# Four GNN layers on one core: the edge sort's unpacking on GpSimd, its tile comparison in bf16 pairs, a class table of its own, two hot rows on VectorE, and another order on TensorE

## The reference

```python
edge_index = jnp.stack([src, dst])
x = x + L0(relu(ln(x)), edge_index, edge_attr_32, edge_type_2, edge_weight)   # attention
x = x + L1(relu(ln(x)), src, dst)                                             # softmax-weighted sum
x = x + L2(relu(ln(x)), edge_index, edge_attr_2)                              # two-layer MLP, batch norm
x = x + L3(relu(ln(x)), edge_index, edge_type_16)                             # message and update
# L2: h = concat([x[row], x[col], edge_attr]) @ W1 + b1, segment_sum over row
# L3: m = relu(concat([x[src], emb[edge_type]]) @ W.T + b), segment_sum over dst
```

## Time and profile before

| | |
|---|---|
| median of 3 runs | 4499.23 us (4487.35 to 4502.24) |
| span of the profiled execution | 4484.2 us |
| the sort's loop in it, first L2859 to the flag | 1888 to 2386 us |
| of these 498 us: PE / DVE / ACT / POOL busy | 311.0 / 461.5 / 384.8 / 0 us |
| granted TensorE clock there, share of 2.4 GHz | 0.77 |

### The profile page before, as it was taken

One profiled execution on the slowest core, in us unless ns is written; L12 is line 12 of the kernel. 1 busy time (PEld: TensorE's weight loads), 2 busy tenths in 40 slices (PEclk: granted clock), 3 DMA queues, 4 the chain that ended last, 5 costly groups with the idle time before them and its releaser, 6 DMA issues.

```text
span 4484.2 us, 86419 instructions
## 1 busy us (share of the span) xinstructions
PE 3388.1 (76%) x31445; PEld 2760.2 (62%) x31445; DVE 3298.9 (74%) x6627; ACT 2085.6 (47%) x6042; POOL 1894.4 (42%) x2179
## 2 busy tenths in 40 slices
PE   1388888778989863266663778868699999869996
PEld 1155555545555542166663678855599999859995
DVE  5477776657777754599995887776766666779997
ACT  2355555545666532288883557660222222234443
POOL 0366677757777751000000210000255555548884
PEclk6688898889999976677876889989899999989998
DMA  4666676667777740100001220114244443223332
GB/s 96 210 189 182 189 201 188 188 165 203 223 210 215 211 119 14 39 9 12 12 10 32 90 68 38 46 46 158 82 126 126 125 127 125 88 68 128 129 128 67
DMA packets 382872, 524.57 MB, mean 117 GB/s; under 512 B 78756, under 2 KB 309862, under 8 KB 382304
## 3 DMA queue, kind: packets, MB, share of 16 engines
q1 hardware_dynamic: 328287, 354.60, 26.1%
q0 software_dynamic: 54144, 164.25, 12.9%
HBM read 407.61 MB, written 111.07 MB: 116 GB/s over the span
## 4 chain that ended last, share of the span: by engine, by line
PE 35%; DVE 28%; POOL 14%; issue 9%; ACT 7%; DMA 3%; another core or an unknown queue 2%; SPq 2%; DVEq 0%; POOLq 0%; ACTq 0%
POOL arena_a L1191 11%; PE psum L3700 5%; PE psum L3716 4%; PE psum L3651 4%; PE psum L3649 4%; PE psum L3003 3%; POOL arena_c L1229 2%; ACT arena_c L2966 2%; PE psum L3616 2%; PE psum L3675 2%; PE psum L3288 2%; PE psum L3698 2%; DVE arena_a L3196 2%; PE psum L3647 2%
## 5 line engine op out<-in xcount | busy, mean ns | idle before, releaser
L1191 POOL DMA_INDIRECT arena_a<-src_table,src_tix x808 | 820.4, 1015 | 459.8 <-issue 380.6
L3420 POOL TENSOR_SCALAR node_hot<-arena_c 128x128 fp32r<-128x128 f32 x575 | 369.4, 653 | 900.7 <-DVE arena_c L3308 568.0
L3438 DVE SCALAR_TENSOR_TENSOR msg_parts<-psum,msg_parts 128x512 fp32r<-128x512 f32 (+2 forms) x644 | 425.2, 660 | 260.5 <-ACT msg_parts L3587 228.3
L3138 POOL TENSOR_SCALAR node_hot_dst<-arena_c 128x128 fp32r<-128x128 f32 x587 | 383.9, 671 | 122.1 <-DVE arena_c L3542 67.6
L3587 ACT ACTIVATE msg_parts<-psum 128x512 fp32r<-128x512 f32 (+2 forms) x325 | 186.4, 574 | 520.6 <-PE psum L3651 520.6
L3003 PE MATMUL psum<-arena_a,arena_c 128*128 128x150 f32 x1800 | 288.7, 330 | 173.7 <-ACT arena_c L2969 173.7
L3649 PE MATMUL psum<-arena_c,arena_a 128*128 128x128 bf16 x3675 | 406.4, 220 | 0.0
L3651 PE MATMUL psum<-arena_c,arena_a 128*128 128x128 bf16 x3675 | 406.4, 220 | 0.0
L3003 PEld LDWEIGHTS psum<-arena_a,arena_c 128*128 128x128 f32 x1800 | 283.1, 224 | 176.8 <-ACT arena_c L2969 176.8
L3128 POOL TENSOR_SCALAR arena_a<-arena_a,arena_c 128x2500 bf16<-128x2500 bf16 x8 | 60.0, 7500 | 709.0 <-DMA arena_a<-bucket_lists 709.0
L1371 ACT ACTIVATE arena_c<-psum 128x272 f32<-128x272 f32 x404 | 151.4, 393 | 432.2 <-remote 233.8
(11 more groups left out here) (594 smaller groups left out, 10190.3 us busy)
## 6 DMA issues: line engine op xcount, KB each, us to landing
y_rows<-arena_c SPq DMA_DIRECT2D x101, 576.0 KB
arena_a<-bucket_rows SPq DMA_DIRECT2D x150, 384.0 KB
arena_b<-near_keys SPq DMA_DIRECT2D x101, 252.0 KB
arena_a<-bucket_rows SPq DMA_DIRECT2D x50, 448.0 KB
arena_a<-bucket_lists SPq DMA_DIRECT2D x25, 896.0 KB
pair_counts<-arena_c SPq DMA_DIRECT2D x25, 800.0 KB
arena_a<-bucket_lists SPq DMA_DIRECT2D x25, 704.0 KB
arena_a<-src_table,src_tix POOLq DMA_INDIRECT x808
```

What stands on the lines that cost most here:

```text
L1191: e.indirect_dma_start(out_, None, table, bass.IndirectOffsetOnAxis(ap=idx, axis=0)).then_inc(sem, 16)
L3138: return e.tensor_scalar(node_hot3[at % RING_H][:, i, :], iota_row, dst_lo[:, b, t:t + 1], None, ALU.is_equal)
L3420: return e.tensor_scalar(node_hot[at % RING_M][:, i, :], iota_row, src_lo[:, b, 2 * k + j:2 * k + j + 1], None, ALU.is_equal)
L3438: e.scalar_tensor_tensor(out=to[:, 1, 0:nt, :], in0=bank[at % 4][:, 0:nt * P].rearrange("p (t f) -> p t f", f=P), scalar=0.0, in1=to[:, 0, ...
```

## The change

Five edits go together.

- `edge_table` has three words an edge (key and two attributes); the class goes to `class_table`. SP writes both, and loads both for each bucket, into `class_in` (dense) and `edge_in`. The comparison with the classes now reads `class_in`.
- The key packs its fields by 512 instead of 256. The comparison that gives `in_tile` takes bf16 inputs and output, in pairs of columns: a new small copy writes each tile number twice (`tile_pair`), and `tile_pairs` holds 1 to 50 in bf16.
- Rows 34 and 35 of `hot_pos` are written by VectorE (an equality, 128x256); ScalarE makes 34 rows and a Relu of 4352 words.
- The unpacking leaves VectorE. ScalarE copies the 150 packed words from PSUM to `packed_sb`, and GpSimd unpacks them (15 operations, division by 512 through rounding in fp32). `turned_pe` is waited for only ahead of GpSimd's last three copies.
- TensorE transposes bucket n-3 after the small products of n and ahead of the 36 products of n-1; before, it transposed n-2 behind the 36 products of n-1. The 36 products wait for `copied`, not `fields`, to reuse their bank.

```diff
-            own.step(e.tensor_tensor(member[s][:, :, 1:], bc(edge_in[b % RING_E][:, :, 0], 1, NB), bc(class_rows[:, b, :], 2, EPP), ALU.is_equal))
+            own.step(e.tensor_tensor(member[s][:, :, 1:], bc(class_in[b % RING_E], 1, NB), bc(class_rows[:, b, :], 2, EPP), ALU.is_equal))
...
-            own.step(e.tensor_tensor(in_tile, bc(tile_i, 2, KT), bc(tile_row, 1, EPP), ALU.is_equal))
+            own.mark(e.tensor_copy(tile_pair, bc(tile_i, 2, 2)))
+            e.tensor_tensor(hot_pos[s][:, ACT_HOT:, :], bc(pos_i[:, ACT_HOT:], 2, P), bc(iota_row, 1, EPP - ACT_HOT), ALU.is_equal)
+            own.settle()
+            own.step(e.tensor_tensor(in_tile.rearrange("p j (k c) -> p j k c", c=2), bc(tile_pair, 2, KT // 2), bc(tile_pairs, 1, EPP), ALU.is_equal))
...
+        def pool_unpack(e, own, b):
+            s = b % 2
+            key, attrs = packed_sb[s][:, 0:KT], packed_sb[s][:, KT:3 * KT].rearrange("p (a k) -> p a k", a=2)
+            rest = attr_rest.rearrange("p (a k) -> p a k", a=2)
+            f, kept = field[s], attr_keep[b]
+            e.wait_ge(sig.copied, b + 1)
+            own.mark(e.tensor_scalar(shifted, key, 1.0 / 512, 8388608.0, ALU.mult, ALU.add))
+            own.step(e.tensor_copy(kept[:, 0:2, :], attrs))
+            own.mark(e.tensor_scalar(above, shifted, -8388608.0, None, ALU.add))
+            own.step(e.tensor_tensor(rest, attrs, kept[:, 0:2, :], ALU.subtract))
+            own.mark(e.tensor_scalar(shifted, above, 1.0 / 512, 8388608.0, ALU.mult, ALU.add))
+            own.mark(e.tensor_scalar(end_lo, above, -512.0, -1.0, ALU.mult, ALU.add))
+            own.step(e.tensor_copy(kept[:, 2:4, :], rest))
+            own.mark(e.tensor_scalar(whole, shifted, -8388608.0, None, ALU.add))
+            own.mark(e.tensor_tensor(dst_lo[:, b, :], end_lo, key, ALU.add))
+            own.mark(e.tensor_tensor(kept[:, 4:6, :], rest, kept[:, 2:4, :], ALU.subtract))
+            own.settle()
+            own.step(e.tensor_scalar(end_hi, whole, -512.0, -1.0, ALU.mult, ALU.add))
+            own.step(e.tensor_tensor(src_lo[:, b, :], end_hi, above, ALU.add))
+            if b >= 2:
+                e.wait_ge(sig.turned_pe, b - 1)
+            e.tensor_copy(f[:, TYP, :], whole)
+            e.tensor_copy(f[:, DL, :], dst_lo[:, b, :])
+            e.tensor_copy(f[:, SL, :], src_lo[:, b, :]).then_inc(sig.fields, 1)
...
+                if 0 <= n - 2 < NB:
+                    b = n - 2
+                    s = b % 2
+                    e.wait_ge(sig.packed_pe, b + 1)
+                    if b >= 2:
+                        e.wait_ge(sig.fields, b - 1)
+                    e.activation(packed_sb[s], bank[2 + s][:, 0:3 * KT], ACT.Copy).then_inc(sig.copied, 1)
```

More of the change, by code:

```diff
@@ L677, in program @@
         restart = words(B_, 2775, [P, NB, EPP + 1])
-        in_tile = words(B_, 3700, [P, EPP, KT])
+        in_tile = words(B_, 3700, [P, EPP, KT], BF16)
+        packed_sb = [words(B_, 4600 + s * 3 * KT, [P, 3 * KT]) for s in range(2)]
+        whole, above, end_lo, end_hi, shifted = (words(B_, 4900 + i * KT, [P, KT]) for i in range(5))
+        tile_pair = words(B_, 5150, [P, EPP, 2], BF16)
+        tile_pairs = words(B_, 5190, [P, KT // 2, 2], BF16)
         RING_E = 4
-        edge_in = [words(B_, 5500 + s * 144, [P, EPP, 4]) for s in range(RING_E)]
+        class_in = [words(B_, 5500 + s * EPP, [P, EPP]) for s in range(RING_E)]
+        edge_in = [words(B_, 5644 + s * 3 * EPP, [P, EPP, 3]) for s in range(RING_E)]
+        ACT_HOT = 34
         tot = [words(B_, 6076 + s * NB, [P, NB]) for s in range(2)]
@@ L2916, in dve_sort @@
             dve_sort_lists(e, own)
-            for n in range(NB + 2):
+            for n in range(NB + 1):
                 if n < NB:
                     dve_classes(e, own, n)
-                if 0 <= n - 1 < NB:
+                if n >= 1:
                     dve_route(e, own, n - 1)
-                if n >= 2:
-                    dve_unpack(e, own, n - 2)
             e.wait_ge(sig.pre_used, NB)
@@ L2951, in pool_sort @@
             pool_gather(e, first_of, dst_keys, begin_i[0], sig.d_keys)
+            for b in range(NB):
+                pool_unpack(e, own, b)
             e.wait_ge(sig.flag, 1)
+        def pool_unpack(e, own, b):
[22 more added lines that the diff above has]
+            e.tensor_copy(f[:, SL, :], src_lo[:, b, :]).then_inc(sig.fields, 1)
         def act_sort(e):
@@ L2964, in act_sort @@
                     e.wait_ge(sig.routed, b + 1)
-                    for j in range(EPP):
+                    for j in range(ACT_HOT):
                         away = e.activation(hot_pos[s][:, j, :], iota_row, ACT.Abs, bias=minus_pos[s][:, j:j + 1])
@@ L2986, in pe_sort @@
             pause(e)
-            for n in range(NB + 2):
+            for n in range(NB + 3):
                 if n < NB:
@@ L2994, in pe_sort @@
                     e.matmul(bank[6 + s][0:1, 0:NB], ones[:, 0:1], tot[s], start=True, stop=True).then_inc(sig.pre_pe, 1)
[L2995 to L3007 removed]
+                if n >= 3:
+                    b = n - 3
                     s = b % 2
@@ L3017, in pe_sort @@
                     t_.then_inc(sig.turned_pe, 1)
+                if 0 <= n - 1 < NB:
+                    b = n - 1
+                    s = b % 2
+                    e.wait_ge(sig.spread, b + 1)
+                    e.wait_ge(sig.weighed, b + 1)
+                    if b >= 2:
+                        e.wait_ge(sig.copied, b - 1)
+                    for j in range(EPP):
+                        put = e.matmul(bank[2 + s][:, 0:3 * KT], hot_pos[s][:, j, :], routed_v[s][:, j, :, :].rearrange("p f k -> p (f k)"),
+                                       start=(j == 0), stop=(j == EPP - 1))
+                    put.then_inc(sig.packed_pe, 1)
             e.wait_ge(sig.flag, 1)
@@ L3756, in gpsimd @@
         def gpsimd(e):
-            pool_constants(e)
+            own = pool_constants(e)
             sp_wait_tables0(e)
```

77 lines of the change are left out of this document (23 added, 54 removed).

## The result

| | before | after |
|---|---|---|
| median of 4 runs | 4500.73 us (4487.35 to 4502.76) | 4426.72 us (4413.70 to 4442.63) |
| ratio after / before | | 0.9844, 95% interval 0.9809 to 0.9879 |
| span of the profiled execution | 4484.2 us | 4411.9 us |
| its part ahead of the sort | 1851.7 | 1837.1 |
| the sort, first fill of its tiles to the flag | 534.7 | 473.8 |

The change is faster, and more so than forecast: 4426.72 us is 33 us under the predicted 4460 and 7 us under the low end of the range. In the profiled execution 60.9 of the 72.3 us come from the sort. Another 14.6 come from layer 0, which the change doesn't touch; the first two experiments measure what that part does on its own.

A forecast was written before the change was run, and what follows sets the result against it. VectorE was taken to bound the sort at 18.75 us a bucket, falling to 15.5 + 1.4 = 16.9; 44.4 us gained less 5.2 lost gives 39, so 4445 for the profiled execution and 4460 for the median, range 4434 to 4492.

The forecast's parts named there:

- What bounded it before: Sort loop before the change: VectorE sets the pace at 18.75 us a bucket, with a ring close behind.
- its ring: Sort, ScalarE's rows, products, small products, VectorE over two buckets: 16.3 us a bucket before, 15.9 after without contention.
- VectorE's parts: VectorE in the sort, a bucket: 18.74 - 2.15 - 0.67 - 0.93 + 0.5 = 15.5 us if undisturbed.
- Contention: Sort, GpSimd meeting VectorE's two-input operations: nine of 15 cost VectorE 0.15 us each, 1.4 us a bucket (0.5 to 3.8).
- its rival that ended slower: Sort: each of nine meetings costs VectorE a whole GpSimd operation, 0.42 us; 19.3 us a bucket, 4517 us, chance 0.09.
- The pace: Sort after the change: VectorE is the limit at 16.9 us a bucket (16.2 to 17.6), chance 0.51.
- the first rival: Sort: no contention worth the name, the ring limits at 15.9 to 16.1 us a bucket; 60 gained, 4439 us, chance 0.18.
- ends of the loop: Sort loop's ends: unhidden unpacking of the last bucket +4.7 us, ahead of the first bucket +0.5; 5.2 us lost.
- GpSimd's operations: Unpacking on GpSimd: 11 operations at 0.39 us and 4 at 0.53, 6.4 us a bucket, 6.6 with semaphore waits.
- its upper figure of 8.8 us: GpSimd's unpacking a bucket if its five two-input operations cost twice as much.
- The sum: Whole kernel: 24 x (18.75 - 16.9) = 44.4 us gained, 5.2 lost, so 39 us gained.
- The signs named beforehand: Sort: L2871 and L2899 at 1.1 us, rows 10.04, products every 16 to 17.5, GpSimd minima near 0.39, VectorE medians 0.1 above minima.

The follow-up runs named there:

- the first two experiments: Kernel before and changed kernel, both unchanged, profiled and timed once more: 4375.73 and 4313.34 us, ratio 0.9856; sorts 534.8 and 471.8 us.
- the kernel in which GpSimd rests: Changed kernel with the same 15 unpacking operations back on VectorE, GpSimd doing nothing in the loop: 4348.92 us, ratio to before 0.9936.
- 27 no more: Changed kernel with GpSimd's 12 arithmetic operations done twice, 27 operations a bucket in place of 15: sort 513.0 us, period 17.72 us.
- one copy on ScalarE that waited for a transpose at the wrong place: Changed kernel with the transposes of bucket n-3 behind the 36 products of n-1: 4652.17 us, sort 718.8 us.

## Why the prediction was right and wrong

**What bounded it before:** right for VectorE, but a second limit was missed. The prediction gave its ring 2.4 us of slack a bucket. Another ring had hardly any: VectorE unpacked bucket b behind b's 36 products and ahead of the route of b+2. The chain of the kernel before runs through it for a while:

```profile
...
1994.18 10.64 ACT arena_c L2966 x36
2004.84 4.05 ACT arena_c L2969
2008.94 12.04 PE psum L3003 x72
2032.12 10.65 ACT arena_c L2966 x36
...
```

Between the end of the products (2021.00) and 2032.12 VectorE unpacks, compares with the classes, and routes. The 37.94 us from 1994.18 to 2032.12 are 19.0 a bucket. From 2109 to 2147 us, with shorter products, the chain is on VectorE with 18.8 us a bucket. The two limits stood side by side, and the change took the unpacking out of both.

**VectorE's parts:** right, to 0.1 us. The class comparison takes 1.09 us undisturbed (forecast 1.10), the tile comparison in bf16 1.09 (1.1), the hot rows 0.43 (0.41), L2902 5.78 (5.78). The sum of 15.5 compares with 15.47 measured, which even has the contention in it. With GpSimd at rest it is 15.14, and some 0.2 to 0.3 us of gaps between instructions come on top (17.29 of 17.56, 16.19 of 16.37 busy where VectorE is the limit).

**Contention:** wrong, and this is the step that failed. Nine meetings at 0.15 us were to cost VectorE 1.4 us a bucket; against the kernel in which GpSimd rests, 15 operations cost it 0.3 and 27 no more. From the one overlap in the earlier trace rows, where GpSimd came first with 7.09 us and VectorE lost 5.5, I took a price for each column, and charged VectorE with it in all nine. The price itself was about right: L2871 loses 0.10 us in the mean and 0.18 at most. The charge was wrong, for the one that waits is the one that comes second. VectorE's operations are long (11.6 us of two-input ones in a bucket) and GpSimd's short (0.23 to 0.38 us), so GpSimd nearly always comes second, and when it doesn't, VectorE can lose no more than the short operation. Nearly all the waiting was on GpSimd, which had it to spare: its turn took 11.5 us (2076.57 to 2088.06) for 4.4 us of work. In the mean GpSimd lost 6.8 us a bucket (11.17 busy for 4.36 of work) and VectorE 0.3.

The Trainium skill's page "SBUF — State Buffer", section "Who interferes with whom", says that whoever comes first keeps the shared ports for the whole instruction and the other fully blocks. The trace agrees: 5.93 us for L2959 behind L2902. The prediction used this rule only for its rival that ended slower, with GpSimd first every time; asked for both orders, it speaks for VectorE.

**The pace:** the forecast had VectorE at 16.9 us as the limit. With nearly no contention it came to 15.5, and the ring was longer: the first rival, given 0.18, which had said 15.9 to 16.1 and 4439 us. Measured are 16.17 and 16.12. That its gain of 60 us is the sort's 60.9 is in part luck: its ring was 0.1 us a bucket too short, which is 3 us, and its ends of the loop 3.5 us too dear. The small rest is in one piece of the ring. I took 11.3 us for the 36 products, between the single row that I read (10.91) and the mean; they took 11.55 in the mean before and 11.75 after. How long a run takes goes with how much of it falls into a stretch at the lower clock, as the runs of 11.41 and 12.49 us above show. The first rival's sum with 11.75 is (10.04 + 3.82 + 11.75 + 0.6 + 6.03) / 2 = 16.1. The runs with 36 and 32 rows on ScalarE and with the fp32 comparison show that it is this ring.

**GpSimd's operations:** too dear. 4.36 us alone (2299.88 to 2304.24, behind the last bucket) in place of 6.6:

```profile
2299.88 0.24 POOL L2950 TENSOR_SCALAR arena_b<-arena_b 128x50 f32<-128x50 f32 x1 [8.38 <-ACT arena_b L2995]
...
2302.52 0.38 POOL L2959 TENSOR_TENSOR arena_c<-arena_a,arena_c 128x100 bf16<-128x100 f32 x1
...
2304.01 0.23 POOL L2967 CAST arena_a<-arena_c 128x50 bf16<-128x50 f32 x1
```

A one-input operation of 50 columns takes 0.23 to 0.35 us and not 0.39, one of 100 columns with two inputs 0.38 and not 0.53; successive independent ones start 0.17 to 0.2 us apart. (Four of the 15 have two inputs; the prediction counted five, which enters only its upper figure of 8.8 us.)

**The ends of the loop:** from the last product to the flag 9.87 us became 11.43, so +1.6 and not +4.7, 2.2 us of the difference being the cheaper operations. Most of the other 0.9 was in SyncE's queue: before, the last bucket's rows lay ready at 2380.41 us, but SyncE was issuing the ten stores of the bucket ahead until 2381.44 and began with the last ones at 2381.48. After, they are ready at 2305.98 and it begins at 2306.00. Ahead of the first product 1.0 us was gained, where I had +0.5.

**The sum:** 24 x (18.78 - 16.17) = 62.6 and 1.0 gained, 1.6 and 1.1 (a slower last run of products) lost: 60.9, where 39 were forecast. With these 60.9 us alone the median would have been 4438, above the low end of 4434; that it came out at 4426.72 is the scatter ahead of the sort. I had put the scatter of the runs at some 8 us; the first comparison alone carries 14.6 us of it there.

**The signs named beforehand:** L2871 and L2899 at 1.1 us, 34 rows in 10.04 us, products every 16 to 17.5 us, no wait of length for `fields` ahead of L3027 (3.8 us in 17 buckets): all as said. GpSimd's minima were lower, its maxima of 5.9 us as said. VectorE's medians above their minima by 0.1 us: no. L2871 has a median of 1118 ns over 1090, L2899 one of 1112 over 1089. That was the sign for the term that failed.

## What to carry to other kernels

Once the busiest engine is relieved, the next limit can be, as here, no engine at all but a ring through double buffers. Add up its pieces with their mean times, not with those of one bucket, and halve for two buffers; giving work to the engine that looks busiest can then help. When two engines share ports, ask for each meeting who comes second: here the short operations beside the long ones lost nearly all of the time themselves (11.5 us for 4.4 us of work), and the engine with the long ones hardly noticed (0.3 us in 15.5). So price the contention on each engine, and see which of them has slack for it. And when a stage is moved a round later, walk every queue that has a piece of it: one copy on ScalarE that waited for a transpose at the wrong place cost 240 us.

## What the runs showed of the hardware

- A GpSimd operation of 50 fp32 columns, 0.24 to 0.35 us alone, takes up to 5.8 us when it meets a VectorE operation with two inputs. VectorE's loss is under 0.2 us in any instruction of the changed kernel's loop, and 0.3 us a bucket in all: 0.10 in L2871, 0.04 in L2899, and 0.10 in L2892, which has one input and takes 0.18 us undisturbed.
- The same 72 instructions of TensorE's products took 11.41 us with the granted clock at 0.50 for the first 4.0 us, and 12.49 with it at 0.50 for the first 6.2.
- A bf16 comparison of 1800 columns takes 1.09 us, 0.61 ns a column, though one input repeats each pair of columns and the other repeats a row of 50. The fp32 form takes 2.08 us here.
- The class comparison, 900 fp32 columns from dense words, takes 1.09 us. From words 16 bytes apart it was 1.77.
- The kernel before took 4500.73, 4375.73, 4457.34 (one run) and 4452.49 us in the four sets of runs, the last three on three different chips. In the two sets in which it was profiled, the sort took 534.7 and 534.8 us, and the 107 us lay ahead of it, in layer 0.
